# Shared second products as a 512- and a 256-column matmul, read out two banks at a time

## The chip, the cores and the metric

One NeuronCore of a Trainium2 chip runs the kernel. The metric is the device time of one execution in microseconds. Three runs of the kernel before took 1114.66, 1115.58 and 1115.99 us; the median is 1115.58 us.

## The reference

`x` has 128 samples of 64 rows and 256 columns. The first half of the work is a gated mixture of three two-layer networks, in float32:

```python
def _dense(x, wi_, wo_):
    return relu(x @ wi_) @ wo_                 # 256 -> 1024 -> 256
s0 = _dense(x, swi[0], swo[0])                 # shared by all samples
s1 = _dense(x, swi[1], swo[1])
eo = relu(x @ wi[type_label]) @ wo[type_label] # one of 5 experts per sample
gate_in = concat([eo[:, 0], s0[:, 0], s1[:, 0]])
w = softmax(relu(gate_in @ g1) @ g2)           # three weights per sample
x = x + eo * w0 + s0 * w1 + s1 * w2
```

The second half adds to `x` a weighted second difference along the columns, one along the rows (both reflected at the edges), and `zR * x * (1 - x)`.

## The kernel before, in words

Every operand of a product is cut into a high part of reduced precision and a low rest, and the product is the sum of high x high, high x low and low x high. So each logical product is three matmuls, or a wide and a narrow one where the high and low part of the moving operand lie side by side.

The work is a row of passes. Passes 0 and 1 compute the gate's inputs, passes 2 to 23 the expert of one group of samples each and store the results to DRAM. From pass `FIRST` = 24 on come the shared passes: tile t (8 samples, 512 rows, t = 0 to 15) has a pass with b = 0 (`s0`) and one with b = 1 (`s1`), and the last one is split into two passes of half width (`HALVES`). A pass has eight chunks c = 0 to 7 of 128 hidden values. Each engine runs its own program over the same sequence of chunks (`for g in range(G + LAG)`), and semaphores tie them together; the order in each queue is the order of the code.

In 29 of the shared passes (`seven(n)`, all but the first two and the half-width ones) the first product of a pair of chunks is done with seven block products in place of eight, from sums of column blocks of `x` and of weights (`seven_step`). The even step of TensorE holds the products `corner`, `side`, `other` and `corner`, the odd step `other`, `corner` and, last, `corner` for the bottom half. ScalarE copies intermediate banks to SBUF, VectorE adds to them. The even chunk is the "top", the odd chunk the "bottom". Its hidden values come from two places: the right half from `LOW_RIGHT` in SBUF, the left half from the corner bank in PSUM. ScalarE writes the high part (`right_high`, `left_high`), VectorE the low part (`right_low`, `left_low`).

The second product of a chunk follows two steps later (`LAG`): four blocks of 128 rows, in groups (0, 1) and (2, 3) between the products above. In an odd step they stand behind `other` and `corner`; only in step c = 1 do blocks 0 and 1 (of chunk 7 of the pass before) stand first. In the shared passes a block's second product is `pair_product`: three matmuls of 256 columns into half a bank, two blocks per bank. A pass uses two of the four result banks, and the passes alternate between the pairs of banks. `add_shared` multiplies a bank by the sample's weight and adds it to `y`, straight from PSUM, 512 columns at a time: in step c = 2 for a finished b = 1 pass, in c = 5 for a finished b = 0 pass. In the expert passes the second product is a matmul of 512 columns and one of 256 into a bank of its own.

Beside this VectorE has one larger task in most steps: `lap_x`, `react`, `add_x`, `lap_y`, `result` of the previous tile in passes with b = 0, and in passes with b = 1 `turn_tile` (c = 0), `residual` (c = 1), `tile_low_whole` (c = 2), `column_sums` and `column_sums_left` (c = 3 and 4, four operations of 256 columns) and `column_sums_low` (c = 6). ScalarE has `tile_high_whole` in c = 1 and `column_sums_high` in c = 5 of these, and `quadratic` in c = 3 of passes with b = 0. GpSimd issues the expert weights' DMAs in the first stage, then makes two sets of weight sums and two small matrices, and is idle until the last block. SyncE's queue issues the other DMAs; `halos` copies rows of `y` between partitions once `add_shared` of the tile is done.

Of the kernel before, what the change touches and what calls it, by code (L numbers as in the profile page):

```python
# [5 lines left out]
F32 = mybir.dt.float32  # L6
# [135 lines left out]
def acc_before(n, u):  # L142
    return max([v for (m, w), v in ACC.items() if m < n and result_bank(m, w) == result_bank(n, u)], default=0)
# [133 lines left out]
def cond_resid_program(nc, x, itok, zx, zy, zr, wi, wo, swi, swo, g1, g2, out):  # L277
    eo_d = nc.dram_tensor("eo_scratch", (NS + NSLOT, S, D), F32, kind="Internal").ap()
    ctx = ExitStack()
    with ctx:  # L280
# [83 lines left out]
        E0 = sb("e0", [128, D])  # L364
        z1 = sb("z1", [128, 2, 128])
# [11 lines left out]
        acc = [ctx.enter_context(nc.psum_tensor(f"acc{i}", [128, 512], F32)) for i in range(4)]  # L377
# [39 lines left out]
        p_hi = sem("p_hi")  # L417
        p_lo = sem("p_lo")
# [33 lines left out]
        P5_ROOM, LOW_RIGHT = gate_room[:, 0:256], later_part[:]  # L452
# [19 lines left out]
        def acc_of(n, j):  # L472

            if paired(n):
                return acc[result_bank(n, j // 2)][:, j % 2 * D:(j % 2 + 1) * D]
            return acc[result_bank(n, j)][:, 0:D]
# [91 lines left out]


# [23 lines left out]
        def _(e):  # L593
# [134 lines left out]
            def column_sums(t):  # L728

                x = [[by_half(XZ[:])[:, k, 2 * h:2 * h + 2, :] for h in range(2)] for k in range(2)]  # L730
                e.wait_ge(xt_lo, t + 1)
                e.tensor_tensor(x[1][1], x[1][1], x[0][1], ALU.subtract).then_inc(*V.up())
                e.wait_ge(dve_seq, V.n)
                e.tensor_tensor(x[0][1], x[0][1], x[0][0], ALU.subtract).then_inc(*V.up())

            def column_sums_left(t):
                x = [[by_half(XZ[:])[:, k, 2 * h:2 * h + 2, :] for h in range(2)] for k in range(2)]
                e.wait_ge(dve_seq, V.n)
                e.tensor_tensor(x[0][0], x[1][1], x[0][0], ALU.add).then_inc(*V.up())
                e.wait_ge(dve_seq, V.n)  # L740
                e.tensor_tensor(x[1][0], x[1][0], x[0][0], ALU.subtract).then_inc(*V.up())
                AT["columns", t] = V.n

# [19 lines left out]
            def right_low(g):  # L763

                e.wait_ge(p_hi, pair_at(g) + 1)
                e.scalar_tensor_tensor(h_slot(HL, g)[:, 256:512], LOW_RIGHT, 0.0,
                                       h_slot(HH, g)[:, 256:512].bitcast(F32), ALU.max, ALU.subtract).then_inc(p_lo, 1)

            def left_low(g):
                n, c = CHUNKS[g]  # L770
                e.wait_ge(h_hi, g + 1 - 2 * NC)
                e.scalar_tensor_tensor(h_slot(HL, g)[:, 0:256], corner_bank(n, c // 2)[:, 0:256], 0.0,
                                       h_slot(HH, g)[:, 0:256].bitcast(F32), ALU.max, ALU.subtract).then_inc(h_lo, 1)
# [17 lines left out]
            def low_right_sum(g):  # L791
                q = pair_at(g)
                e.wait_ge(p_copy, 4 * q + 4)
                e.tensor_tensor(LOW_RIGHT, LOW_RIGHT, P5_ROOM, ALU.add).then_inc(p_sum, 1)  # L794
# [79 lines left out]
            def add_shared(n):  # L874

                t, b = PASSES[n][1] // 2, PASSES[n][1] % 2
                for u in results(n):
                    y = inner(t)[:, 2 * u:2 * u + 2, :]
                    e.wait_ge(acc_done, ACC[n, u])
                    if b == 0:  # L880
                        e.wait_ge(dve_seq, AT["residual", t])
                    else:
                        e.wait_ge(acc_free, ACC[n - 1, u])
                    e.scalar_tensor_tensor(y, acc[result_bank(n, u)][:].rearrange("p (j d) -> p j d", j=2),
                                           WB[:, 1 + b, t:t + 1], y, ALU.mult, ALU.add).then_inc(acc_free, 1)
# [49 lines left out]
            def shared_sum(j):  # L935
# [3 lines left out]
                e.wait_ge(acc_free, ACC[NP - 3, j // 2])  # L939
                e.scalar_tensor_tensor(y, acc_of(NP - 2 + j % 2, j), WB[:, 2, NT - 1:NT], y, ALU.mult, ALU.add).then_inc(*V.up())  # L940
# [73 lines left out]
            for g in range(G + LAG):  # L1014
# [20 lines left out]
                if (n, c) == (FIRST, 7):  # L1035
                    e.wait_ge(t_prod, T_AT["hidden"])
                    e.tensor_scalar(z1[:].rearrange("p a n -> p (a n)"), tbank[:, 0:256], 0.0, None,
# [8 lines left out]
                if g < G and c == 0 and seven(n - 1) and not seven(n):  # L1046
                    right_low(g - 1)
                    left_low(g - 1)
# [32 lines left out]
                if FIRST <= n < NP - 1:  # L1081
                    t, b = PASSES[n][1] // 2, PASSES[n][1] % 2
                    if b == 0 and t >= 1:
# [17 lines left out]
                    if b == 1 and t < NT - 1:  # L1101
# [29 lines left out]
        def _(e):  # L1131
# [240 lines left out]
            def pair_product(n, j, c):  # L1372
# [3 lines left out]
                to = acc_of(n, j)  # L1376
                if c == 0 and j % 2 == 0:
                    e.wait_ge(acc_free, acc_before(n, j // 2))
                e.matmul(to, hi, woc[:, f, 0:D], start=(c == 0 and j % 2 == 0), stop=False, skip_group_check=True)  # L1379
                e.matmul(to, hi, woc[:, f, D:2 * D], start=False, stop=False, skip_group_check=True)  # L1380
                return e.matmul(to, lo, woc[:, f, 0:D], start=False, stop=(c == NC - 1 and j % 2 == 1),  # L1381
                                skip_group_check=True)

            def half_product(n, j, c):
# [3 lines left out]
                to = acc_of(n, j)  # L1388
# [73 lines left out]
        def _(e):  # L1462
# [31 lines left out]
            def column_sums_high(t):  # L1494
                e.wait_ge(dve_seq, AT["columns", t])
# [11 lines left out]
            def right_high(g):  # L1507
# [3 lines left out]
                e.activation(h_slot(HH, g)[:, 256:512], LOW_RIGHT, ACT.Relu).then_inc(p_hi, 1)  # L1511

            def left_high(g):
                n, c = CHUNKS[g]
                e.wait_ge(h_prod, g + 1)
                e.wait_ge(*h_free(g - NH))
                e.activation(h_slot(HH, g)[:, 0:256], corner_bank(n, c // 2)[:, 0:256], ACT.Relu).then_inc(h_hi, 1)
# [6 lines left out]
            def seven_step(g):  # L1524
# [4 lines left out]
                if c % 2 == 0:  # L1529
# [4 lines left out]
                    if q >= 1:  # L1534
                        right_high(g - 1)
# [4 lines left out]
                    if q >= 1:  # L1540
                        left_high(g - 1)
# [4 lines left out]
                if q >= 1:  # L1546
                    e.wait_ge(p_lo, q)
                e.activation(LOW_RIGHT, corner, ACT.Copy).then_inc(p_copy, 1)  # L1548
                top_high(g - 1)

            def evacuate(n):
                i = PASSES[n][1]
                for j in block_order(n):
# [3 lines left out]
                    e.activation(EO[i % 2][:, j, :], acc[j][:, 0:D], ACT.Copy).then_inc(acc_hi, 1)  # L1557

# [361 lines left out]
```

## Time and profile before

| | |
|---|---|
| median of three runs | 1115.58 us |
| the profiled execution | 1114.96 us |
| its span | 1113.5 us |
| TensorE busy | 1105.2 us, 99%, 8004 matmuls |
| VectorE busy | 819.9 us, 74% |
| ScalarE busy | 593.9 us, 53% |
| GpSimd busy | 89.4 us, 8% |
| granted clock, mean | 0.998 |

The span runs from the first to the last instruction; about 1.5 us of the execution lie outside it. Busy time is a share of the whole span, so an engine can be busier than that in one stage. A matmul's recorded time covers its way through the array and overlaps the next one's; what a matmul costs in a full stream is the distance between two starts. A row's bracket tells how long the engine was idle before it and what released it. hh and hl are the high and low parts of the hidden values, swo and ewo the second weights, acc the result banks, first_part and gT the rooms of the tops, later_part the bottom's right half.

### The profile page before, as it was taken

Reading aid. Unit: us, or ns where it says so; the run is one execution under the profiler, and the core shown is the slowest. Engines: PE = TensorE matmul, PEld = TensorE weight load, DVE = VectorE, ACT = ScalarE, POOL = GpSimd, SP = SyncE. Lnnn points to the kernel's source line nnn. Section 1 sums busy time; section 2 is a strip of 40 time slices with the busy share of each in tenths; the row PEclk is TensorE's granted clock in tenths of the full one; section 3 lists DMA queues with packets and bytes.
Section 4 is the critical chain, followed back from the end, with each engine's and each line's share of the span. In section 5 each row is a group of like instructions: output and inputs, shape, how many; then the busy total and the mean of one; then the engine's idle time right before and its main releaser. Section 6 shows DMA issues by size and latency. Waiting matters only on the chain.

```text
span 1113.5 us, 22306 instructions
## 1 busy us (share of the span) xinstructions
PE 1105.2 (99%) x8004; PEld 1044.5 (94%) x8004; DVE 819.9 (74%) x1459; ACT 593.9 (53%) x1265; POOL 89.4 (8%) x131
## 2 busy tenths in 40 slices
PE   9999999999999999999999999999999999999998
PEld 8888888888888888999999999999999999999998
DVE  5665666666666644787788788787787887877876
ACT  3554555555565532455555555555555555555552
POOL 1211212121121104000000000000000000000001
PEclk9999999999999999999999999999999999999999
DMA  8555656555564425220220221211212212212100
GB/s 271 181 164 180 188 189 195 183 172 169 187 204 147 146 51 165 62 76 32 61 65 30 77 48 50 77 43 56 77 40 58 77 36 62 77 33 64 59 30 25
DMA packets 112368, 114.28 MB, mean 103 GB/s; under 512 B 78505, under 2 KB 87298, under 8 KB 112258
## 3 DMA queue, kind: packets, MB, share of 16 engines
q1 hardware_dynamic: 97826, 61.74, 19.2%
q0 software_dynamic: 13952, 50.60, 14.2%
q8 instruction: 63, 1.03, 0.4%
q10 hardware_dynamic: 480, 0.53, 0.2%
q14 instruction: 47, 0.39, 0.1%
HBM read 91.49 MB, written 17.04 MB: 97 GB/s over the span
## 4 chain that ended last, share of the span: by engine, by line
PE 99%; DVE 1%; issue 0%; ACT 0%; POOL 0%; DVEq 0%; POOLq 0%
PE acc L1380 11%; PE acc L1381 11%; PE acc L1379 11%; PE acc L1365 10%; PE hbank L1286 6%; PE hbank L1287 6%; PE hbank L1229 6%; PE hbank L1230 6%; PE hbank L1231 6%; PE hbank L1288 6%; PE acc L1366 5%; PE tbank L1287 2%; PE tbank L1286 2%; PE tbank L1288 2%; PE acc L1267 1%; PE acc L1342 1%
## 5 line engine op out<-in xcount | busy, mean ns | idle before, releaser
L1380 PE MATMUL acc<-swo,hh 128*128 128x256 f32 x992 | 280.5, 283 | 0.0
L1381 PE MATMUL acc<-swo,hl 128*128 128x256 f32 x992 | 280.2, 282 | 0.0
L1379 PE MATMUL acc<-swo,hh 128*128 128x256 f32 x992 | 279.9, 282 | 0.0
L859 DVE SCALAR_TENSOR_TENSOR hl<-hbank,hh 128x512 fp32r<-128x512 f32 (+1 forms) x184 | 111.7, 609 | 147.6 <-ACT hh L1492 147.4
L1492 ACT ACTIVATE hh<-hbank 128x512 fp32r<-128x512 f32 (+1 forms) x184 | 98.0, 535 | 190.5 <-PE hbank L1231 189.3
L1380 PEld LDWEIGHTS acc<-swo,hh 128*128 128x128 f32 x992 | 189.1, 191 | 0.6
L1381 PEld LDWEIGHTS acc<-swo,hl 128*128 128x128 f32 x992 | 189.5, 191 | 0.0
L1379 PEld LDWEIGHTS acc<-swo,hh 128*128 128x128 f32 x992 | 188.7, 190 | 0.7
L1365 PE MATMUL acc<-ewo,hh 128*128 128x512 f32 x496 | 179.9, 394 | 0.0
L1366 PE MATMUL acc<-ewo,hl 128*128 128x256 f32 x496 | 139.0, 280 | 0.0
L1365 PEld LDWEIGHTS acc<-ewo,hh 128*128 128x128 f32 x496 | 93.1, 188 | 21.1
L1229 PE MATMUL hbank<-xh,ewh 128*128 128x512 f32 (+1 forms) x288 | 107.3, 372 | 0.0
L1230 PE MATMUL hbank<-xl,ewh 128*128 128x512 f32 (+1 forms) x288 | 104.7, 364 | 0.0
L1231 PE MATMUL hbank<-xh,ewl 128*128 128x512 f32 (+1 forms) x288 | 104.3, 362 | 0.0
L1366 PEld LDWEIGHTS acc<-ewo,hl 128*128 128x128 f32 x496 | 93.4, 188 | 4.2
L794 DVE TENSOR_TENSOR later_part<-later_part,gT 128x256 f32<-128x256 f32 x116 | 49.2, 424 | 25.8 <-ACT later_part L1548 24.8
L1548 ACT ACTIVATE later_part<-hbank 128x256 f32<-128x256 f32 x58 | 22.4, 385 | 81.3 <-PE hbank L1288 81.3
L1229 PEld LDWEIGHTS hbank<-xh,ewh 128*128 128x128 f32 x288 | 54.1, 188 | 10.0
L1231 PEld LDWEIGHTS hbank<-xh,ewl 128*128 128x128 f32 x288 | 54.1, 188 | 9.5
L1230 PEld LDWEIGHTS hbank<-xl,ewh 128*128 128x128 f32 x288 | 54.5, 189 | 4.5
L890 DVE TENSOR_TENSOR ewo<-rw,ewo 128x1024 fp32r<-128x1024 f32 x44 | 53.5, 1217 | 2.4 <-ACT ewo L1574 2.4
L1751 POOL TENSOR_TENSOR ss<-y 128x254 f32<-128x254 f32 x3 | 1.8, 609 | 663.2 <-DVE y L940 663.2
(325 smaller groups left out, 2752.4 us busy)
## 6 DMA issues: line engine op xcount, KB each, us to landing
rw<-in_L_cond_wi POOLq DMA_DIRECT2D x44, 512.0 KB, 4.6
rw<-in_L_cond_wo POOLq DMA_DIRECT2D x44, 512.0 KB, 4.6
eo_scratch<-eo SPq DMA_DIRECT2D x128, 64.0 KB, 2.2
rw<-in_x SPq DMA_DIRECT2D x256, 32.0 KB, 2.2
xs<-in_x SPq DMA_DIRECT2D x16, 512.0 KB, 3.5
ei<-eo_scratch SPq DMA_DIRECT2D x16, 512.0 KB, 4.3
xs<-in_x SPq DMA_DIRECT2D x126, 64.0 KB, 3.3
out<-ot SPq DMA_DIRECT2D x15, 512.0 KB, 2.7
```

The costliest lines, as they stand in the source:

```text
L859: e.scalar_tensor_tensor(h_slot(HL, g), bank[:, 0:w], 0.0, h_slot(HH, g).bitcast(F32), ALU.max, ALU.subtract).then_inc(h_lo, 1)
L1229: e.matmul(to, wh[:, k, cs], xh[k], start=(k == 0), stop=False)
L1230: e.matmul(to, wh[:, k, cs], xl[k], start=False, stop=False)
L1231: i = e.matmul(to, wl[:, k, cs], xh[k], start=False, stop=(k == 1))
L1286: e.matmul(to, hi, cols[0], start=start, stop=False, skip_group_check=True)
L1287: e.matmul(to, hi, cols[1], start=False, stop=False, skip_group_check=True)
L1365: e.matmul(acc[j][:, 0:2 * D], HH[:, g % NH, at], woc[:, f, :], start=(c == 0), stop=False)
L1366: m = e.matmul(acc[j][:, D:2 * D], HL[:, g % NH, at], woc[:, f, 0:D], start=False, stop=last)
L1379: e.matmul(to, hi, woc[:, f, 0:D], start=(c == 0 and j % 2 == 0), stop=False, skip_group_check=True)
L1380: e.matmul(to, hi, woc[:, f, D:2 * D], start=False, stop=False, skip_group_check=True)
L1381: return e.matmul(to, lo, woc[:, f, 0:D], start=False, stop=(c == NC - 1 and j % 2 == 1), skip_group_check=True)
L1492: e.activation(h_slot(HU if upright(g) else HH, g), bank_of(g)[:, 0:w], ACT.Relu).then_inc(h_hi, 1)
```

## The change

- `pair_product` issues two matmuls per block in place of three, of 512 and 256 columns, into a bank of its own. A shared pass so fills all four banks, and chunk 0 of the next pass waits until they are read out.
- The read-out has two steps for two banks at a time: `shared_high` on ScalarE copies the high columns, scaled, to `EOS` (in the room of `g1s`); `shared_low` on VectorE adds the scaled low columns. They run in steps c = 1 and c = 2 of the next pass. `add_shared` now adds `EOS` to `y` in SBUF, 1024 columns at once, in the steps where it stood.
- The bottom's hidden values are gathered in one SBUF room `LOW` of 512 columns: ScalarE copies the left half there and cuts the whole with one Relu (`bottom_high`), VectorE makes the low part in one operation (`bottom_low`). Both stand where `left_high` and `left_low` stood.
- `column_sums` moves from VectorE to GpSimd.
- On GpSimd the second set of weight sums moves behind the wait for the gate's hidden values and the two small matrices.
- Waits for the end of `add_shared` (`lap_x`, `quadratic`, `halos`) are on VectorE's own counter.

```diff
-def result_bank(n, u):
-    if paired(n):
-        return 2 * ((n - FIRST) % 2) + u
-    if n in HALVES:
-        return {0: 2, 2: 3, 1: 0, 3: 1}[u]
-    return u
+def result_banks(n, u):
+    return {2 * u, 2 * u + 1} if paired(n) else {u}
 def acc_before(n, u):
-    return max([... if m < n and result_bank(m, w) == result_bank(n, u)], default=0)
+    return max([... if m < n and result_banks(m, w) & result_banks(n, u)], default=0)
...
+        P5_ROOM, LOW = later_part[:], ez[:]
+        def acc_part(u, part):
+            return acc_all[:, 2 * u:2 * u + 2, part * D:(part + 1) * D]
+        EOS = g1s[:, 1:5, :]
...  VectorE
-            def right_low(g): ...
-            def left_low(g): ...
+            def bottom_low(g):
                 e.wait_ge(h_hi, g + 1 - 2 * NC)
+                e.scalar_tensor_tensor(h_slot(HL, g), LOW, 0.0, h_slot(HH, g).bitcast(F32),
+                                       ALU.max, ALU.subtract).then_inc(h_lo, 1)
             def seven_step(g):
                 if c % 2 == 0:
                     top_left_sum(g)
                     if pair_at(g) >= 1:
-                        right_low(g - 1)
-                        left_low(g - 1)
+                        bottom_low(g - 1)
                     return
                 top_right_sum(g)
+                if c == 1:
+                    shared_low(n - 1, 0)
                 low_right_sum(g)
                 top_low(g - 1)
+            def shared_low(n, u):
+                t, b = PASSES[n][1] // 2, PASSES[n][1] % 2
+                e.wait_ge(acc_hi, ACC[n, u] - 2)
+                if (t, b) != (0, 0):
+                    e.wait_ge(dve_seq, AT["shared", t + b - 1, 1 - b])
+                e.scalar_tensor_tensor(EOS[:, 2 * u:2 * u + 2, :], acc_part(u, 1), WB[:, 1 + b, t:t + 1],
+                                       EOS[:, 2 * u:2 * u + 2, :], ALU.mult, ALU.add).then_inc(acc_free, 1)
             def add_shared(n):
-                for u in results(n):
-                    ...
-                    e.scalar_tensor_tensor(y, acc[...], WB[:, 1 + b, t:t + 1], y, ...).then_inc(acc_free, 1)
+                e.wait_ge(acc_free, ACC[n, 1])
+                e.wait_ge(dve_seq, AT["residual", t] if b == 0 else AT["shared", t, 0])
+                e.tensor_tensor(inner(t), inner(t), EOS, ALU.add).then_inc(*V.up())
...  VectorE's order
+                if FIRST < n < NP - 1 and c == 2:
+                    shared_low(n - 1, 1)
                 if g < G and seven(n):
                     seven_step(g)
...
+                    if n > FIRST and not seven(n) and c == 1:
+                        shared_low(n - 1, 0)
...
-                        if c == 3:
-                            column_sums(t + 1)
-                        if c == 4:
-                            column_sums_left(t + 1)
...  TensorE, pair_product
-                e.matmul(to, hi, woc[:, f, 0:D], start=(c == 0 and j % 2 == 0), stop=False, ...)
-                e.matmul(to, hi, woc[:, f, D:2 * D], start=False, stop=False, ...)
-                return e.matmul(to, lo, woc[:, f, 0:D], start=False, ...)
+                e.matmul(acc[j][:, 0:2 * D], hi, woc[:, f, :], start=(c == 0), stop=False)
+                return e.matmul(acc[j][:, D:2 * D], lo, woc[:, f, 0:D], start=False, stop=(c == NC - 1))
...  ScalarE
-            def right_high(g): ...
-            def left_high(g): ...
+            def bottom_high(g):
+                e.wait_ge(h_prod, g + 1)
+                e.activation(LOW[:, 0:256], corner_bank(n, c // 2)[:, 0:256], ACT.Copy).then_inc(p_left, 1)
+                e.wait_ge(p_left, q + 1)
+                e.wait_ge(p_sum, 3 * q + 3)
+                e.wait_ge(*h_free(g - NH))
+                e.activation(h_slot(HH, g), LOW, ACT.Relu).then_inc(h_hi, 1)
             def seven_step(g):
                     e.activation(TOP[q % 2][:, 0:256], corner, ACT.Copy).then_inc(p_copy, 1)
-                    if q >= 1:
-                        right_high(g - 1)
                     ...
                     e.activation(P5_ROOM, other, ACT.Copy).then_inc(p_copy, 1)
                     if q >= 1:
-                        left_high(g - 1)
+                        bottom_high(g - 1)
+            def shared_high(n, u):
+                e.wait_ge(acc_done, ACC[n, u])
+                if (t, b) == (0, 0):
+                    e.wait_ge(t_free, T_AT["spread"])
+                else:
+                    e.wait_ge(dve_seq, AT["shared", t + b - 1, 1 - b])
+                e.activation(EOS[:, 2 * u:2 * u + 2, :], acc_part(u, 0), ACT.Copy,
+                             scale=WB[:, 1 + b, t:t + 1]).then_inc(acc_hi, 1)
...  ScalarE's order
+                if FIRST < n < NP - 1 and c in (1, 2):
+                    shared_high(n - 1, c - 1)
                 if g < G and seven(n):
                     seven_step(g)
...  GpSimd
+            weight_sums(0)
             e.wait_ge(t_free, T_AT["hidden"])
             ... the two small matrices ...
+            weight_sums(1)
+            for t in range(1, NT):
+                column_sums(t)    # four tensor_tensor of 256 columns, each behind the one before
...  SyncE
             def halos(t):
-                e.wait_ge(acc_free, ACC[FIRST + 2 * t + 1, 1])
+                e.wait_ge(dve_seq, AT["shared", t, 1])
```

## Rows read from the trace of the kernel before

**Rows 1.** The page: TensorE's busy time, and the chain of waits by engine.
```profile
PE 1105.2 (99%) x8004; PEld 1044.5 (94%) x8004; DVE 819.9 (74%) x1459; ACT 593.9 (53%) x1265; POOL 89.4 (8%) x131
...
PE 99%; DVE 1%; issue 0%; ACT 0%; POOL 0%; DVEq 0%; POOLq 0%
```
**Rows 2.** Busy us (instructions) of PE, PEld, DVE, ACT, POOL; clock, DMA share, GB/s.
```profile
520.00:1060.00 540.00, 540.00 (x4539) 540.00 (x4538) 446.37 (x835) 304.22 (x745) 0.00 (x0) 1.00 0.20 57
```
**Rows 3.** Timeline, TensorE, an expert pass: start, duration (us), line, operands.
```profile
301.26 0.40 PE L1365 MATMUL acc<-ewo,hh 128*128 128x512 f32 x1
...
302.65 0.40 PE L1229 MATMUL hbank<-xh,ewh 128*128 128x512 f32 x1
```
**Rows 4.** Timeline, TensorE, from pass b = 0 into b = 1.
```profile
697.02 0.28 PE L1288 MATMUL hbank<-th,suml 128*128 128x256 f32 x1
...
698.92 0.28 PE L1379 MATMUL acc<-swo,hh 128*128 128x256 f32 x1
...
699.52 0.28 PE L1381 MATMUL acc<-swo,hl 128*128 128x256 f32 x1
...
702.51 0.28 PE L1379 MATMUL acc<-swo,hh 128*128 128x256 f32 x1
...
703.58 0.28 PE L1379 MATMUL acc<-swo,hh 128*128 128x256 f32 x1
```
**Rows 5.** Timeline, ScalarE, the same stretch.
```profile
697.34 0.39 ACT L1539 ACTIVATE gT<-hbank 128x256 f32<-128x256 f32 x1
697.62 0.38 ACT L1517 ACTIVATE hh<-tbank 128x256 fp32r<-128x256 f32 x1
...
700.84 0.62 ACT L1522 ACTIVATE hh<-first_part 128x512 fp32r<-128x512 f32 x1
701.36 1.06 ACT L1484 ACTIVATE xh<-rw 128x1024 fp32r<-128x1024 f32 x1
```
**Rows 6.** Timeline, VectorE, the same stretch.
```profile
698.03 0.42 DVE L772 SCALAR_TENSOR_TENSOR hl<-tbank,hh 128x256 fp32r<-128x256 f32 x1
...
700.27 0.42 DVE L789 TENSOR_TENSOR first_part<-hbank,first_part 128x256 f32<-128x256 f32 x1 [0.66 <-PE hbank L1288]
...
701.49 0.69 DVE L760 SCALAR_TENSOR_TENSOR hl<-first_part,hh 128x512 fp32r<-128x512 f32 x1
702.10 1.28 DVE L897 SCALAR_TENSOR_TENSOR y<-ei,wb,xs 128x1024 f32<-128x1024 f32 x1
```
**Rows 7.** Groups by form: busy us, mean ns, idle before. ScalarE 100:440, VectorE 520:1060.
```profile
L1492 ACT ACTIVATE hh<-hbank 128x512 fp32r<-128x512 f32 x94 | 56.1, 601 | 110.8 <-PE hbank L1231 110.5
...
L884 DVE SCALAR_TENSOR_TENSOR y<-acc,wb,y 128x512 f32<-128x512 f32 x50 | 35.1, 743 | 0.0
...
L923 DVE TENSOR_TENSOR ss<-y 128x1024 f32<-128x1024 f32 x13 | 15.8, 1216 | 0.0
...
L732 DVE TENSOR_TENSOR rw<-rw 128x256 f32<-128x256 f32 x13 | 5.4, 419 | 0.0
```
**Rows 8.** Timeline, GpSimd and VectorE at the end of the kernel.
```profile
1105.60 0.61 POOL L1751 TENSOR_TENSOR ss<-y 128x254 f32<-128x254 f32 x1 [4.06 <-DVE y L940]
1105.63 0.87 DVE L980 SCALAR_TENSOR_TENSOR qq<-y,sm,qq 128x256 f32<-128x256 f32 x1
...
1106.75 0.47 DVE L980 SCALAR_TENSOR_TENSOR qq<-y,wb,qq 128x256 f32<-128x256 f32 x1
```
**Rows 9.** Timelines, VectorE and TensorE, the gate's weights.
```profile
435.95 2.66 DVE L832 TENSOR_SCALAR wx<-mask,vals 128x16 f32<-128x16 f32 x3
...
438.75 0.43 PE L1432 MATMUL tbank<-wx,selb 128*128 128x96 f32 x2 [2.26 <-DVE wx L832]
```
**Rows 10.** Timelines, the halo copies of one tile (SP's queue) and their reader.
```profile
683.73 0.56 SPq L1820 DMA_DIRECT2D y<-y  x1
...
690.42 0.59 SPq L1832 DMA_DIRECT2D y<-y  x1
...
693.02 1.22 DVE L923 TENSOR_TENSOR ss<-y 128x1024 f32<-128x1024 f32 x1
```

More of the change, by code:

```diff
@@ L142, in acc_before @@
 def acc_before(n, u):
-    return max([v for (m, w), v in ACC.items() if m < n and result_bank(m, w) == result_bank(n, u)], default=0)
+    return max([v for (m, w), v in ACC.items() if m < n and result_banks(m, w) & result_banks(n, u)], default=0)
 def tile_parts(n, c):
@@ L363, in cond_resid_program @@
         g1s = sb("g1s", [128, 6, D])
-        E0 = sb("e0", [128, D])
-        z1 = sb("z1", [128, 2, 128])
+        ez = sb("ez", [128, 2 * D])
+        E0, z1 = ez[:, 0:D], ez[:, D:2 * D].rearrange("p (a n) -> p a n", a=2)
         selb = sb("selb", [128, 128])
@@ L376, in cond_resid_program @@
         tbank = ctx.enter_context(nc.psum_tensor("tbank", [128, 512], F32))
-        acc = [ctx.enter_context(nc.psum_tensor(f"acc{i}", [128, 512], F32)) for i in range(4)]
+        acc_all = ctx.enter_context(nc.psum_tensor("acc", [128, 4, 512], F32))
+        acc = [acc_all[:, i, :] for i in range(4)]
         h_prod = sem("h_prod")
@@ L416, in cond_resid_program @@
         p_sum = sem("p_sum")
-        p_hi = sem("p_hi")
-        p_lo = sem("p_lo")
+        p_left = sem("p_left")
+        x_sum = sem("x_sum")
         raw_in = [sem(f"raw_in{i}") for i in range(2)]
@@ L726, in tile_low_whole @@
                                 ALU.subtract).then_inc(xt_lo, 1)
[L728 to L742, printed above, removed]
             def column_sums_low(t):
@@ L793, in low_right_sum @@
                 e.wait_ge(p_copy, 4 * q + 4)
-                e.tensor_tensor(LOW_RIGHT, LOW_RIGHT, P5_ROOM, ALU.add).then_inc(p_sum, 1)
+                e.tensor_tensor(LOW[:, 256:512], LOW[:, 256:512], P5_ROOM, ALU.add).then_inc(p_sum, 1)
             def seven_step(g):
@@ L872, in evacuate @@
                     e.tensor_tensor(dst, acc[j][:, D:2 * D], dst, ALU.add).then_inc(acc_free, 1)
+            def shared_low(n, u):
[5 more added lines that the diff above has]
+                                       EOS[:, 2 * u:2 * u + 2, :], ALU.mult, ALU.add).then_inc(acc_free, 1)
             def add_shared(n):
                 t, b = PASSES[n][1] // 2, PASSES[n][1] % 2
-                for u in results(n):
[L878 to L885, printed above, removed]
+                e.wait_ge(acc_free, ACC[n, 1])
+                e.wait_ge(dve_seq, AT["residual", t] if b == 0 else AT["shared", t, 0])
+                e.tensor_tensor(inner(t), inner(t), EOS, ALU.add).then_inc(*V.up())
+                AT["shared", t, b] = V.n
             def cut_low(ws, p):
@@ L938, in shared_sum @@
                 e.wait_ge(acc_done, ACC[NP - 2 + j % 2, j])
-                e.wait_ge(acc_free, ACC[NP - 3, j // 2])
-                e.scalar_tensor_tensor(y, acc_of(NP - 2 + j % 2, j), WB[:, 2, NT - 1:NT], y, ALU.mult, ALU.add).then_inc(*V.up())
+                e.wait_ge(dve_seq, AT["shared", NT - 1, 0])
+                e.scalar_tensor_tensor(y, acc[j][:, 0:D], WB[:, 2, NT - 1:NT], y, ALU.mult, ALU.add).then_inc(*V.up())
                 AT["last", j] = V.n
@@ L1494, in column_sums_high @@
             def column_sums_high(t):
-                e.wait_ge(dve_seq, AT["columns", t])
+                e.wait_ge(x_sum, 4 * t)
                 if t >= 3:
@@ L1588, in quadratic @@
             def quadratic(t):
-                e.wait_ge(acc_free, ACC[FIRST + 2 * t + 1, 1])
+                e.wait_ge(dve_seq, AT["shared", t, 1])
                 if t == 0:
@@ L1722, in _, with weight_sums @@
                             EO[u % 2][b:128:k, 0:k // 2, :]).then_inc(last_out, 16)
-            for i in range(2):
+            def weight_sums(i):
                 top, bottom = W_RAW[i]
@@ L1734, in _, with column_sums @@
                 e.tensor_tensor(top[:, 1, :], top[:, 1, :], top[:, 0, :], ALU.subtract).then_inc(w_sum, 1)
+            def column_sums(t):
+                x = [[by_half(XZ[:])[:, k, 2 * h:2 * h + 2, :] for h in range(2)] for k in range(2)]
+                e.wait_ge(xt_lo, t + 1)
+                e.tensor_tensor(x[1][1], x[1][1], x[0][1], ALU.subtract).then_inc(x_sum, 1)
+                e.wait_ge(x_sum, 4 * t - 3)
+                e.tensor_tensor(x[0][1], x[0][1], x[0][0], ALU.subtract).then_inc(x_sum, 1)
+                e.wait_ge(x_sum, 4 * t - 2)
+                e.tensor_tensor(x[0][0], x[1][1], x[0][0], ALU.add).then_inc(x_sum, 1)
+                e.wait_ge(x_sum, 4 * t - 1)
+                e.tensor_tensor(x[1][0], x[1][0], x[0][0], ALU.subtract).then_inc(x_sum, 1)
+            weight_sums(0)
             e.wait_ge(t_free, T_AT["hidden"])
@@ L1823, in halos @@
             def halos(t):
-                e.wait_ge(acc_free, ACC[FIRST + 2 * t + 1, 1])
+                e.wait_ge(dve_seq, AT["shared", t, 1])
                 shifted(t)
```

43 lines of the change are left out of this document (9 added, 34 removed).

## The prediction

> **What bounds the kernel now.** I read the page first: TensorE is busy 99% of the span and the chain of waits ends on it for 99% [rows 1]. Then busy time by stretch: from 520 to 1060 us TensorE starts 4539 matmuls in 540.00 us without a hole, all of 256 columns, so one costs 119 ns; VectorE is busy 83%, ScalarE 56%, GpSimd 0%, and the granted clock is 1.00, the 2.4 GHz level [rows 2]. So a shorter matmul stream shortens the kernel one for one, but only as long as each wait inside it is met in time. So the timelines of TensorE, ScalarE and VectorE around one change of pass decide: what is ready when, and by how much before it is used [rows 4 to 6].
>
> **Fewer matmuls.** A shared second product is three matmuls of 256 columns: 3 x 119 = 357 ns. The new pair, 512 and 256 columns, already exists in the expert passes: four pairs take 302.65 - 301.26 = 1.39 us, 348 ns each [rows 3]. That saves 9 ns on each of 31 passes x 8 chunks x 4 blocks = 992: **-8.9 us**. (Bounds from the rounding of these rows: -7 to -11.)
>
> The Trainium skill (TensorE: Matmul & The Clock Gate, "Wait — 56ns, not 53.3ns?") puts the fixed cost of a warm matmul at about 2.5 ns. One matmul less would then save 2.5 us in all. The rows say 9 ns and I follow them.
>
> **The bottom half of the hidden values.** Before, ScalarE cut the right half early (L1511) and the left half (L1517) right after the copy of `other` (L1539); VectorE's L772 ended at 698.03 + 0.42 = 698.45, and TensorE used the result at 698.92 [rows 4 to 6]. After, everything follows the copy of `other`: a copy of the left half to SBUF, a 512-column Relu that waits for that copy on its own engine, a 512-column subtraction, and only then TensorE. The chain starts when the matmul of 697.02 ends, 697.30:
> - ScalarE copy of `other` from 697.34 [rows 5]; the next one 0.28 later, 697.62, takes 0.38: 698.00.
> - Relu over 512 columns, 0.62 as L1522 [rows 5], after a step of 0.04: 698.66.
> - VectorE over 512 columns, 0.69 as L760 [rows 6], after a step of 0.03: 699.38.
> - to the first matmul 0.14: L832 ends at 435.95 + 2.66 = 438.61 and its reader starts at 438.75 [rows 9]. Ready 699.52.
>
> TensorE wants it at 698.92, less four blocks x 9 ns: 698.88. In step c = 1 the blocks 0 and 1 of the previous pass's last chunk stand first in the queue, so TensorE stops for 0.64 us. Of 29 seven-product passes 28 follow another one: 28 x 0.64 = **+17.9 us**. In the other odd steps six matmuls stand ahead (0.71): wanted 699.59, margin 0.07, which I count as no stall. Bounds: if a dependent step overlapped as independent ones do and the wide operations cost no more than narrow ones, the chain would be some 0.6 shorter and nothing would be lost; if each of four steps is 0.05 longer, it is 0.84 per pass and 0.13 in each of 87 other pairs.
>
> **One set of result banks.** Before, passes alternated between two pairs of banks and the read-out had a pass of time. After, each pass fills all four, so chunk 0 of the next pass must wait for ScalarE's copy and VectorE's multiply-add of banks 0,1 and of banks 2,3. In TensorE's queue blocks 2,3 of chunk 0 stand 703.58 - 698.92 = 4.66 after the blocks above, 4.60 with faster pairs. Behind the new start 699.52 they are wanted at 704.12. Into a pass with b = 1:
> - banks 0,1 done: the row of 699.52 lies 0.60 after 698.92, with pairs 0.58; plus 0.28: 700.38. ScalarE copies 512 columns in 0.60 [rows 7]: 701.02.
> - VectorE: `top_right_sum` (L789, 700.27 [rows 6], later by the stall's 0.60 and earlier by two pairs) 700.85 to 701.27, first read-out (0.74 [rows 7]) to 701.93, `low_right_sum` to 702.27, L760's work 702.19 to 702.88; each starts 0.08 before the last one ends, as 701.49 + 0.69 against 702.10 shows [rows 6]. Then `residual`, 1.28 [rows 6], to 704.08, and only then the second read-out, 704.00 to 704.74; with 0.14: 704.88.
>
> ScalarE's second copy, behind L1484 (1.06 [rows 5]), ends near 703.5 and is not the last. Stall 0.76 us; of such passes there are 14: **+10.6 us**. Banks 0,1 (wanted 703.07, free 701.93) are in time. Into a pass with b = 0 there is no `residual`: the second read-out ends at 703.54, no stall. What is queued behind that wait is all of TensorE, and nothing of another engine gains. Bounds: 0, if VectorE is ahead by the length of `residual`; 1.3 per pass if it comes one 0.7 operation later.
>
> **VectorE's load.** Per tile it gains two additions of 1024 columns (2 x 1.22), loses four column sums (4 x 0.42) [rows 7] and in eight pairs trades 2 x 0.42 for 0.69: 2.4 - 1.7 - 1.2 = -0.5 us of 43. Its busy time falls a little, but in each pair it stands about 1 us at the head of its queue waiting for the Relu, where L766 and L772 were. With two additions of 1.2 to 1.3 per pair it is then full, with 0.05 to 0.1 to spare; I count nothing, it belongs to the range.
>
> **Column sums on GpSimd.** Four operations of 256 columns at about 0.61 to 0.72 end long before ScalarE reads them, so they replace VectorE's for free. But while GpSimd ran L1751 from 1105.60 to 1106.21, VectorE's L980, which reads two SBUF tensors, took 0.87; alone it took 0.47 [rows 8]. So such an operation stands until GpSimd's has ended. In c = 3 the 512-column subtraction, with some 0.4 of slack, is held 0.6: 0.2 lost per tile, x 14 = **+2.8 us**. Bounds: 0; four holds of 0.6 with nothing to cover them, 34.
>
> The Trainium skill (SBUF — State Buffer, "Who interferes with whom") says the same: a VectorE instruction with two SBUF inputs and a GpSimd one that reads SBUF exclude each other for a whole instruction. By that rule, the trace agrees.
>
> **The two ends of the shared stage.** The second set of weight sums now stands behind a wait and the small matrices. In the trace the gate's three L832 take 2.66 us beside GpSimd's sums and TensorE waits 2.26 for them [rows 9]; I expect -2.3. Against it, the first read-out, in pass 25: ScalarE has a copy, a Relu (0.60 each) and three casts of 1.06 ahead of the second copy; wanted 1.9 and 3.4 us after banks 0,1 are done, free at 2.7 and 5.5: stalls 0.7 + 2.1. Net **+0.5**. Into the first half-width pass (a chunk there is 12 matmuls): banks 0,1 wanted at 1.25, free at 2.17; banks 2,3 wanted 0.36 later, free at 4.03 behind `residual`: **+2.4**. Bounds for both: -2 and +6.
>
> **Hidden.** The halo copies now start behind the addition instead of the read-out, some 0.7 us later against TensorE. The last is issued 690.42 - 683.73 = 6.7 after the first, and L923 reads them at 693.02 [rows 10]; the stalls give back 0.6 to 1.4 of it. Zero.
>
> **Sum.** -8.9 + 17.9 + 10.6 + 2.8 + 0.5 + 2.4 = +25.3. The profiled execution took 1114.96 us (span 1113.5), 0.6 below the median 1115.58; so the median should become **1141 us**.
>
> **Rivals.**
> - *Faster.* The bottom chain is under 1.58 us (it was 1.3 in the old order, worked out 2.22), so that 698.88 is met: no 17.9, and VectorE, free 0.6 earlier in each pair, does `residual` in time. Left: -8.9 + 0.5 + 2.4 = -6.0: 1110. For it: dependent operations might overlap. Against it: L1517 ends at 698.00 and its reader L772 starts at 698.03 [rows 5, 6], and the two 512-column operations alone take 1.31.
> - *Only the bottom chain.* VectorE runs ahead by more than 0.76 and the read-out is hidden: 1115.6 + 14.7 = 1130. For it: VectorE idles before L789 at 700.27 for 0.66 [rows 6]. Against it: the chain above leaves that idle time in and is still late.
> - *VectorE full.* The margins of 0.05 to 0.1 in the other pairs don't hold; 0.1 in each of 87 is +8.7, with the longer steps at each pass +5: 1155. For it: 83% busy before and a new 1 us wait per pair. Against it: when it is late, the Relu is already done and the wait vanishes.
> - *The saving fails to show.* In this stream, between 256-column products, the pair costs what three matmuls cost, 357 ns, and the stalls stay: 1141 + 8.9 = 1150. For it: 119 ns is itself measured only among 256-column matmuls. Against it: the expert passes hold the same pair at 348. The page's fixed cost, cited above, stands on this side.
>
> **Numbers.** Forecast 43%, with its own range 1135 to 1148; only the bottom chain 16%; VectorE full 27%; no saving 4%; faster 8%; 2% for an unforeseen near-zero. Range 1124 to 1160. A change under 0.2% (2.2 us) can't be told from none here: faster 0.08, same 0.02, slower 0.90.
>
> **What would show it.** Right: TensorE idle before the first second product of step c = 1 by about 0.6, released by VectorE's 512-column subtraction; before the third block of chunk 0 in b = 1 passes by about 0.8, released by the read-out behind `residual`; four new matmul pairs in 1.39 us; two-input VectorE operations of 1.2 us beside GpSimd's sums. Wrong: TensorE without holes in the shared stage, or holes in every pair.

## The result, and the profile after

| | before | after |
|---|---|---|
| median (lowest to highest), us | 1115.12 (1113.49 to 1115.99) | 1151.97 (1151.12 to 1152.39) |
| span of the profiled execution, us | 1113.5 | 1149.6 |

The ratio is 1.0331, with an interval of 1.0313 to 1.0349: the change costs 36.9 us. The forecast was 1141, a cost of 25.3. The direction and the place of the large holes came out as forecast, the size 11 us too small: 1152 lies above the forecast's own range (1135 to 1148).

The page of after, TensorE's row and the others', and the chain of waits by engine:
```profile
PE 1120.6 (97%) x7012; PEld 996.3 (87%) x7012; DVE 823.0 (72%) x1314; ACT 660.2 (57%) x1327; POOL 140.7 (12%) x191
...
PE 85%; DVE 6%; ACT 3%; issue 3%; SPq 1%; DMA 1%; POOLq 0%; DVEq 0%; POOL 0%; ACTq 0%
```
There are 992 matmuls fewer than in [rows 1]; the chain now leaves TensorE for 15% of its length. The stretches (columns as in [rows 2]) tell where: the first line is the start of the shared stage, the second its body, which had no hole before.
```profile
439.00:453.00 14.00, 8.36 (x30) 6.22 (x29) 10.35 (x15) 5.68 (x8) 5.76 (x5) 0.76 0.25 38
...
520.00:1060.00 540.00, 527.66 (x3570) 478.24 (x3570) 429.49 (x676) 344.78 (x762) 40.11 (x48) 1.00 0.20 54
```
In the body 12.3 of 540 us are idle. The waits, over the whole span (waiting engine and line, releaser, total us, count, longest):
```profile
DVE hl L747 <- ACT hh L1490: 71.0, 94, 1.2
...
PEld acc L1356 <- DVE hl L747: 19.8, 28, 0.7
...
PE acc L1356 <- DVE hl L747: 10.6, 28, 0.4
...
PE acc L1356 <- DVE g1s L856: 9.4, 16, 4.0
PEld acc L1356 <- DVE g1s L856: 8.7, 15, 2.1
```
The 28 waits for the 512-column subtraction (L747, `bottom_low`) and the 14 for the read-out (L856) in the body are the two forecast. VectorE itself stood idle before that subtraction 94 times, waiting for ScalarE's Relu (L1490). A wait is also split here between weight load and matmul, so the sums are not holes; below, holes are differences between starts of matmuls.

From the two traces I took the time at which the last second product of each pass starts, and how much later it is after than before:

| stretch | forecast, us | after minus before, us |
|---|---|---|
| up to the start of the shared stage | 0 | +0.1 |
| the gate's weights | -2.3 | -4.2 |
| the first read-out | +2.8 | +8.23 |
| each of 14 passes b = 0 | +0.64 - 0.29 = +0.35 | +0.58 |
| each of 14 passes b = 1 | +0.64 + 0.76 + 0.2 - 0.29 = +1.31 | +1.38 |
| these 28 together | +23.2 | +27.45 |
| into the half-width passes | +2.4 | +0.19 + 3.94 |

0.29 is the forecast for a pass's 32 pairs; the -0.9 of the three other passes belongs to the lines around them. The right column sums to 35.7; the spans differ by 36.1 and the medians by 36.9.

**The bottom chain.** ScalarE, VectorE and TensorE of after, from a b = 0 pass into a b = 1 pass (as [rows 4 to 6]):
```profile
800.87 0.39 ACT L1510 ACTIVATE later_part<-hbank 128x256 f32<-128x256 f32 x1 [0.32 <-PE hbank L1266]
801.15 0.38 ACT L1486 ACTIVATE ez<-tbank 128x256 f32<-128x256 f32 x1
801.56 0.64 ACT L1490 ACTIVATE hh<-ez 128x512 fp32r<-128x512 f32 x1
```
```profile
802.22 0.69 DVE L747 SCALAR_TENSOR_TENSOR hl<-ez,hh 128x512 fp32r<-128x512 f32 x1 [0.22 <-ACT hh L1490]
```
```profile
802.08 0.40 PE L1356 MATMUL acc<-swo,hh 128*128 128x512 f32 x1
802.32 0.28 PE L1357 MATMUL acc<-swo,hl 128*128 128x256 f32 x1
802.97 0.49 PE L1356 MATMUL acc<-swo,hh 128*128 128x512 f32 x1 [0.37 <-DVE hl L747]
803.30 0.28 PE L1357 MATMUL acc<-swo,hl 128*128 128x256 f32 x1
```
The copy (0.38), the Relu (0.64) and the subtraction (0.69) run one behind the other. Without the wait the third matmul would start at 802.44, 0.12 after the one before. It starts 0.53 later, and its partner comes 0.33 after it instead of 0.24: 0.10 more. That is 0.63, against 0.64 forecast.

**The read-out.** The same pass 5 us on, VectorE and then TensorE:
```profile
806.33 1.28 DVE L876 SCALAR_TENSOR_TENSOR y<-ei,wb,xs 128x1024 f32<-128x1024 f32 x1
807.53 0.74 DVE L856 SCALAR_TENSOR_TENSOR g1s<-acc,wb,g1s 128x512 f32<-128x512 f32 x1
```
```profile
808.33 0.50 PE L1356 MATMUL acc<-swo,hh 128*128 128x512 f32 x1 [0.27 <-DVE g1s L856]
808.67 0.28 PE L1357 MATMUL acc<-swo,hl 128*128 128x256 f32 x1
```
`residual` (L876) stands ahead of the second read-out, as forecast. This hole is 0.43 + 0.10. Three matmuls ahead of it, at 807.44, another of 0.08 + 0.10 was not forecast: ScalarE's copy out of the bank that this matmul writes comes late (14 such waits in the trace, for L1506), because the 1024-column `tile_high_whole` (L1459, 1.05) and its second read-out copy (0.68) stand ahead of it. Together 0.71, against 0.76.

**The port.** By this the text means that VectorE's operations with two SBUF inputs and GpSimd's operations hold each other up. GpSimd's column sums, with the VectorE operations that run beside them:
```profile
810.54 0.74 POOL L1722 TENSOR_TENSOR rw<-rw 128x256 f32<-128x256 f32 x1 [41.23 <-DVE xl L722]
811.36 0.80 POOL L1724 TENSOR_TENSOR rw<-rw 128x256 f32<-128x256 f32 x1
812.24 1.06 POOL L1726 TENSOR_TENSOR rw<-rw 128x256 f32<-128x256 f32 x1
```
```profile
805.40 0.41 DVE L769 TENSOR_TENSOR ez<-ez,later_part 128x256 f32<-128x256 f32 x1
805.73 0.68 DVE L741 SCALAR_TENSOR_TENSOR hl<-first_part,hh 128x512 fp32r<-128x512 f32 x1
...
810.71 0.85 DVE L769 TENSOR_TENSOR ez<-ez,later_part 128x256 f32<-128x256 f32 x1
811.49 1.21 DVE L741 SCALAR_TENSOR_TENSOR hl<-gT,hh 128x512 fp32r<-128x512 f32 x1
```
The same two lines of VectorE take 0.41 and 0.68 when GpSimd is quiet, and 0.85 and 1.21 beside it. TensorE loses 0.10 + 0.10 by the second: 0.2, as forecast, though half of it is the slower start behind a hole and not the wait.

### The profile page after: what moved, and what is told of

It reads as the page before. It is cut to its first block, busy times and chain, and to the rows that moved or that the text cites. A ratio compares the mean times of both kernels' runs of the same rounds, so it can differ in the third digit from the quotient of the medians.

```text
span 1149.6 us, 20274 instructions
## 1 busy us (share of the span) xinstructions
PE 1120.6 (97%) x7012; PEld 996.3 (87%) x7012; DVE 823.0 (72%) x1314; ACT 660.2 (57%) x1327; POOL 140.7 (12%) x191
## 4 chain that ended last, share of the span: by engine, by line
PE 85%; DVE 6%; ACT 3%; issue 3%; SPq 1%; DMA 1%; POOLq 0%; DVEq 0%; POOL 0%; ACTq 0%
PE acc L1356 17%; PE acc L1343 10%; PE acc L1357 8%; PE hbank L1207 6%; PE hbank L1208 6%; PE hbank L1209 6%; PE hbank L1264 5%; PE hbank L1266 5%; PE hbank L1265 5%; PE acc L1344 5%; PE tbank L1264 2%; PE tbank L1265 2%; PE tbank L1266 2%; DVE g1s L856 2%; DVE hl L747 2%
## 5 line engine op out<-in xcount | busy, mean ns | idle before, releaser
L1356 PE MATMUL acc<-swo,hh 128*128 128x512 f32 x992 | 374.8, 405 | 20.1 <-DVE hl L747 10.6
L1356 PEld LDWEIGHTS acc<-swo,hh 128*128 128x128 f32 x992 | 186.8, 188 | 62.9 <-DVE hl L747 19.8
L747 DVE SCALAR_TENSOR_TENSOR hl<-ez,hh 128x512 fp32r<-128x512 f32 x116 | 80.3, 692 | 72.3 <-ACT hh L1490 71.0
L1722 POOL TENSOR_TENSOR rw<-rw 128x256 f32<-128x256 f32 x15 | 12.0, 799 | 586.7 <-DVE xl L722 586.7
L1490 ACT ACTIVATE hh<-ez 128x512 fp32r<-128x512 f32 x116 | 73.5, 634 | 3.7
L1537 ACT ACTIVATE g1s<-acc,wb 128x512 f32<-128x512 f32 x62 | 42.4, 685 | 52.5 <-PE acc L1357 46.0
L1510 ACT ACTIVATE later_part<-hbank 128x256 f32<-128x256 f32 x116 | 44.7, 385 | 28.5 <-PE hbank L1266 28.5
L741 DVE SCALAR_TENSOR_TENSOR hl<-gT,hh 128x512 fp32r<-128x512 f32 x58 | 47.4, 817 | 16.1 <-ACT hh L1495 16.1
```

The costliest lines, as they stand in the source:

```text
L747: e.scalar_tensor_tensor(h_slot(HL, g), LOW, 0.0, h_slot(HH, g).bitcast(F32), ALU.max, ALU.subtract).then_inc(h_lo, 1)
L1356: e.matmul(acc[j][:, 0:2 * D], hi, woc[:, f, :], start=(c == 0), stop=False)
```

## The experiments

Each changes after, unless it says before. Their reference runs are of the kernel before on the same chip. What a pass costs is again read from the starts of its last second product, against before.

**e1: the bottom in two halves again, the rest of the change kept.**
```diff
...  VectorE, seven_step (and the same at the pass behind the last of these)
-                        bottom_low(g - 1)
+                        right_low(g - 1)
+                        left_low(g - 1)
...  ScalarE, seven_step (likewise)
+                    if q >= 1:
+                        right_high(g - 1)
...
-                        bottom_high(g - 1)
+                        left_high(g - 1)
```
`right_high` cuts `LOW[:, 256:512]` behind the copy of the corner, `left_high` the bank's 256 columns behind the copy of `other`.

> The changed kernel with the bottom's hidden values cut in two halves again (right_high, left_high, right_low, left_low as before); all else as changed. Holes theory: the 0.64 us hole before the first second product of step c = 1 goes in 28 passes, -17.9; the read-out hole behind residual stays at about 0.6 in 14 passes: 1133 us. Rival, VectorE full: the holes are VectorE being behind, so the 1 us per pair that it no longer waits for the Relu removes the read-out holes too: 1122 us.

Measured: 1128.70, ratio 1.0127 (1.0106 to 1.0147). A miss, halfway between the two expectations. By the medians 23.3 us of the 36.9 hang on the bottom chain (22.4 by the starts in the traces): more than the 17.9 that its 28 holes make up. A b = 0 pass went from +0.58 to -0.26, which is 0.63 for the hole and about 0.2 for small ones in the other steps; a b = 1 pass went from +1.38 to +0.69. That makes 21.4 in the 28 passes; the half-width passes lost 1.9 less. The read-out's holes stay, where *VectorE full* expected them to go. The waits that stay on the second products are those of the read-out and of the start:
```profile
PE acc L1365 <- DVE g1s L864: 9.6, 16, 4.1
PEld acc L1365 <- DVE g1s L864: 8.9, 15, 2.1
```

**e6: the reverse, before with the new bottom alone.** The edit is e1's turned round, in the kernel before, with the rooms of after: `LOW` is `ez`, the copy of `other` goes to `later_part`.

> The kernel before with only the new way to cut the bottom's hidden values (one room, one Relu, one subtraction). Holes theory: a hole of 0.60 + 0.04 us in 28 passes and nothing else: +18, 1133 us. Rival, VectorE full: the 1 us per pair of waiting for the Relu meets an engine at 83%, holes in many pairs: 1140 us or more. Rival, no effect by itself: 1115 us.

Measured: 1135.06, ratio 1.0175 (1.0159 to 1.0190): +19.8. With all matmuls narrow and the old read-out, the same holes appear:
```profile
PEld acc L1370 <- DVE hl L765: 15.9, 28, 0.6
...
PE acc L1370 <- DVE hl L765: 10.2, 28, 0.4
```
```profile
795.28 0.69 DVE L765 SCALAR_TENSOR_TENSOR hl<-ez,hh 128x512 fp32r<-128x512 f32 x1 [0.27 <-ACT hh L1506]
```
```profile
795.27 0.28 PE L1371 MATMUL acc<-swo,hh 128*128 128x256 f32 x1
795.39 0.28 PE L1372 MATMUL acc<-swo,hl 128*128 128x256 f32 x1
...
796.03 0.38 PE L1370 MATMUL acc<-swo,hh 128*128 128x256 f32 x1 [0.36 <-DVE hl L765]
```
796.03 is 0.52 later than 795.39 + 0.12. So the chain alone carries the largest loss. A b = 1 pass costs 0.61 here, a b = 0 pass 0.81: the small losses of after's b = 0 passes come with the chain too. There are 28 large holes, and no hole in every pair: *VectorE full* is refuted for this part.

**e2: `residual` moved out from ahead of the read-out.**
```diff
-                        if c == 1:
+                        if c == (4 if t < NT - 1 else 3):
                             residual(t)
```


> The changed kernel with residual moved from step c = 1 to c = 4 (c = 3 in the last tile), behind the second read-out. Holes theory: the hole before block 2 of chunk 0 (0.43 + 0.10 us) goes in 14 passes, -7.4, and 1 to 3 us go at the first half-width pass; the hole of c = 1 stays: 1142 us. Rival, VectorE full: the same work at another place, at most 2 us: 1150 us.

Measured: 1148.66, ratio 1.0303 (1.0282 to 1.0324). A miss: 3.3 us came back instead of some 10. And these are at the end: into the half-width passes the cost fell from 3.94 to 1.30, while each b = 1 pass still costs 1.39. The third block of chunk 0 is nearly in time, but the hole stands one pair later. TensorE and VectorE of e2:
```profile
808.02 0.50 PE L1356 MATMUL acc<-swo,hh 128*128 128x512 f32 x1
...
812.83 0.50 PE L1356 MATMUL acc<-swo,hh 128*128 128x512 f32 x1 [0.31 <-DVE hl L741]
```
```profile
811.56 1.22 DVE L741 SCALAR_TENSOR_TENSOR hl<-gT,hh 128x512 fp32r<-128x512 f32 x1
```
The subtraction held by GpSimd (1.22) is the same as in after, and there TensorE came only 0.10 too early for it. What changed is TensorE: no longer stopped for `residual`, it comes 0.4 us sooner to a result that is ready at the same time.

**e3: the column sums back on VectorE**, in c = 3 and c = 4 as before, `residual` as in after.
```diff
+                        if c == 3:
+                            column_sums(t + 1)
+                        if c == 4:
+                            column_sums_left(t + 1)
...  GpSimd
-            for t in range(1, NT):
-                column_sums(t)
```


> The changed kernel with the column sums back on VectorE in steps c = 3 and 4. Port theory: VectorE's operations with two SBUF inputs are no longer held by GpSimd's, the 0.2 us hole per tile goes: -2.9, and 0.5 at the first tile: 1149 us. Rival, VectorE full: 1.7 us more work per tile for an engine without room, 0.3 to 1 us per tile: 1156 to 1166 us.

Measured: 1148.15, ratio 1.0295 (1.0273 to 1.0318), close to the 1149 expected. A b = 1 pass costs 1.16 to 1.23 instead of 1.37 to 1.41; 0.2 over 14 is 2.8 us, the port's forecast. The intervals of e3 and after touch, so the total alone would not settle it; the 14 equal passes do.

**e5: e2 with the column sums left out.**
```diff
                         if c == (4 if t < NT - 1 else 3):
                             residual(t)
...  ScalarE, column_sums_high
-                e.wait_ge(x_sum, 4 * t)
+                e.wait_ge(xt_lo, t + 1)
...  GpSimd
-            for t in range(1, NT):
-                column_sums(t)
```


> The kernel with the late residual (e2), and the column sums left out altogether (one part of the computation is missing). Two causes for one hole: the run with the late residual had its hole of 0.53 us before block 2 of chunk 0 replaced by one of 0.57 in c = 4, behind VectorE's subtraction of c = 3, which GpSimd's column sums held from 0.69 to 1.22. Theory: either cause alone keeps the hole, without both it is gone: 14 x 0.6 less than 1148.7, so 1140 us. Rival, VectorE is full at c = 3 whatever GpSimd does: 1147 us.

Measured: 1142.18, ratio 1.0238 (1.0222 to 1.0253). Now a b = 1 pass costs 0.87. The subtraction that was held takes its usual time:
```profile
808.45 0.69 DVE L740 SCALAR_TENSOR_TENSOR hl<-gT,hh 128x512 fp32r<-128x512 f32 x1 [0.36 <-ACT hh L1494]
```
Moving `residual` alone brought nothing per pass, removing the port's conflict alone 0.2, both together 0.5 (0.6 was expected). Two late results overlap here: each covers for the other. What is left in a b = 1 pass is the bottom's 0.63 and about 0.35 behind ScalarE's late copies, less the shorter pairs.

**e4: before with only the second weight sums moved behind the gate.**
```diff
-            for i in range(2):
+            def weight_sums(i):
                 ...
+            weight_sums(0)
             e.wait_ge(t_free, T_AT["hidden"])
             ... the two small matrices ...
+            weight_sums(1)
```


> The kernel before with one part of the change: the second set of weight sums on GpSimd behind the wait for the gate's hidden values and the two small matrices. Port theory: VectorE's three small L832-type operations take 0.2 instead of 0.9 us each, TensorE's wait of 2.26 us goes, and with it the 3.4 us at half clock (1.7 us): 1111.5 us. Rival: the wait was set by something else, no change: 1115.5 us.

Measured: 1111.69 against 1114.45, ratio 0.9977 (0.9967 to 0.9987), in 12 runs. The three L832 of [rows 9] (2.66) shrink, and the stretch behind them, here in before and then in e4, is at full clock:
```profile
439.00:443.50 4.50, 4.50 (x21) 4.08 (x21) 3.84 (x9) 2.28 (x3) 1.72 (x5) 0.62 0.14 23
```
```profile
436.81 0.55 DVE L832 TENSOR_SCALAR wx<-mask,vals 128x16 f32<-128x16 f32 x3
```
```profile
439.00:443.50 4.50, 4.50 (x32) 4.12 (x31) 0.95 (x1) 2.50 (x3) 3.74 (x3) 1.00 0.18 27
```
21 matmuls started in 4.5 us before, 32 now. So the gate's wait cost its 2.26 us and about 4.5 x 0.38 = 1.7 more in clock (from 440 to 442 it was 0.50, the 1.2 GHz level), together 4.0, and by the starts in the two traces pass 24 is 4.0 shorter; the prediction took only the first. The next pass gives 0.4 back. The medians differ by 2.8 only. Before's 17 runs are not alike: those with a mean clock of 1.000 took 1112.2 to 1112.9 us, the others up to 1117.4 at 0.997. So some may not have lost the clock at the gate; only one is in a trace.

**c3 and c4: what the experiments point to.** Kept from the change: the wide pairs, the two-step read-out, the order at the gate. Undone: the new bottom, the column sums on GpSimd. Moved: `residual` to c = 5 and the addition of the b = 0 pass to c = 7; in the first shared passes, the transpose `turn_tile` to c = 1, behind the copy of the gate's weights, and the casts of the weight sums to c = 3. c4 also gives ScalarE's `tile_high_whole` and what depends on it one step more:
```diff
-                        if c == 1:
+                        if c == (5 if t < NT - 1 else 3):
                             residual(t)
...
-                        if c == 0:
+                        if c == (1 if t == 0 else 0):
                             turn_tile(t + 1)
...  c4 alone, ScalarE and then VectorE
-                    c == (2 if n == FIRST + 1 else 1): tile_high_whole
+                    c == 2: tile_high_whole
...
-                        if c == 2:
+                        if c == (2 if t == 0 else 3):
                             tile_low_whole(t + 1)
-                        if c == 3:
+                        if c == (3 if t == 0 else 4):
                             column_sums(t + 1)
```


> A version from the runs: the matmul pair, the two-step read-out and the gate order of the changed kernel; the bottom in two halves and the column sums on VectorE as before; residual in c = 5 and add_shared of b = 0 passes in c = 7; at the first read-out the transposition behind the gate's weights, the casts of the weight sums behind the read-out. Theory: passes with b = 0 gain 0.22 us each, with b = 1 0.03, the start of the shared stage 2 and its end loses 1: 1110 us. Rival: the read-out finds another engine late and the 0.5 us holes stay: 1118 us.

> c3 with ScalarE's tile_high_whole in step c = 2, behind the second read-out, in place of c = 1, tile_low_whole in c = 3 and both halves of the column sums in c = 4 (first tile as in c3). In c3 a pass with b = 1 still has holes of 0.09 + 0.10 and 0.05 + 0.10 us behind ScalarE's late copies. Theory: these go and all passes gain 0.22: 14 x 0.4 less than c3's 1113.2, 1107.6 us. Rival: VectorE, with 1.2 and 1.7 us in neighbouring steps, is late there and the holes move: 1113 us.

Measured: c3 1113.21 against 1115.24, ratio 0.9984 (0.9975 to 0.9993), 3 us short of the 1110 expected, a b = 1 pass at +0.16 in place of -0.03; c4 1108.53 against 1114.89, ratio 0.9946 (0.9933 to 0.9960). c4 is faster than both kernels, and than e4. Its body:
```profile
520.00:1060.00 540.00, 540.00 (x3770) 501.73 (x3769) 467.08 (x866) 340.65 (x803) 0.00 (x0) 1.00 0.21 57
```
TensorE is full again, with 200 more matmuls started than in after. VectorE is busy for 467 us, 38 more than in after, and TensorE waits for none of it. In c4 the b = 1 passes went from c3's +0.16 to -0.18 against before. The wait that c3 has between 520 and 1060 us, and c4 has not, is for ScalarE:
```profile
PEld tbank L1292 <- ACT gT L1536: 3.2, 13, 0.3
```
So the slack for ScalarE's cast is the likely cause; VectorE's `tile_low_whole` and `column_sums` moved with it, and no run separates them.

## Why the forecast was right in direction and short in size

**Where the total fell.** 1152 is nearest to the 1155 of *VectorE full*, but e1, e6 and the waits above refute its cause. The holes are the forecast's own; what it got wrong is above all the two ends.

**Fewer matmuls: -8.9 forecast, 7 to 8 us gained.** Four pairs of the shared stage in after:
```profile
820.62 0.39 PE L1356 MATMUL acc<-swo,hh 128*128 128x512 f32 x1
...
822.02 0.28 PE L1264 MATMUL tbank<-th,swh 128*128 128x256 f32 x1
```
1.40 us against 12 x 0.119 = 1.43: 7 ns each. The b = 0 passes of e1 and c4, which have no large holes, are 0.24 to 0.28 shorter than before, for 32 pairs: about 8 ns. So *the saving fails to show* is refuted. The figure of the Trainium skill (TensorE: Matmul & The Clock Gate, "Wait — 56ns, not 53.3ns?"), about 2.5 ns for a warm matmul, would give a third of what was measured; the rows decide.

**The bottom half: +17.9 forecast, 28 x 0.63 = 17.6 measured.** The chain's steps come out at 2.14 instead of 2.22 (shorter steps), and the restart of the matmul stream adds 0.10 that I had not counted; the two cancel. That the sum hit is in part luck. *Faster* and *only the bottom chain* fall with e1, e6 and the read-out's hole.

**The margin of 0.07 in the other pairs didn't quite hold.** In b = 0 passes 0.05 and 0.10 are lost in c = 3 and less elsewhere, about 0.2 a pass, and what is left of b = 1 passes is 0.1: some 4 us in all, of which I had counted nothing but had named the size (0.1 in each of 87 would be 8.7). *VectorE full* was wrong in its cause: VectorE waited for the Relu before 94 of these subtractions, and with the new bottom alone (e6) the same 0.2 appear. The chain is late by itself.

**The read-out behind `residual`: +10.6 forecast, 14 x 0.71 = 9.9 measured**, of which 0.18 has another cause (ScalarE). The prediction took 0.60 for ScalarE's scaled copy from a Relu's row; it takes 0.69. As a removable cost it is nothing: e2.

**The port: +2.8 forecast, 2.8 by e3.** The number hit by luck: [rows 8] show 0.40 more (0.87 against 0.47) and not 0.6, the subtraction was held 0.53 (1.21 against 0.68), and of the 0.2 lost 0.10 is the slower start behind the hole, which the prediction didn't have. GpSimd's operations lengthen too, 0.74 to 1.06. The Trainium skill (SBUF — State Buffer, "Who interferes with whom") says that a VectorE instruction with two SBUF inputs contends with a GpSimd instruction that reads SBUF; the trace agrees, with 1.21 against 0.68. For the total it matters only where someone waits for the one held.

**The start: +0.5 forecast, +4.02 measured.** This is the term that failed most. The step read "stalls 0.7 + 2.1" for the first read-out; it was 4.0 and 1.6 of waiting and then half the clock. VectorE, ScalarE and TensorE of after:
```profile
440.68 1.24 DVE L717 STREAM_TRANSPOSE rw<-rw 128x1024 f32<-128x1024 f32 x1 [4.24 <-DMA rw<-in_x]
441.85 0.22 DVE L813 COPY wb<-tbank 128x96 f32<-128x96 f32 x1
```
```profile
442.16 0.69 ACT L1537 ACTIVATE g1s<-acc,wb 128x512 f32<-128x512 f32 x1 [6.51 <-DVE wb L813]
```
```profile
444.86 0.47 PE L1356 MATMUL acc<-swo,hh 128*128 128x512 f32 x1 [4.04 <-DVE g1s L856]
447.59 0.80 PE L1356 MATMUL acc<-swo,hh 128*128 128x512 f32 x1 [1.60 <-DVE g1s L856]
```
ScalarE's copy scales by the gate's weights WB. VectorE copies WB out of a bank behind `turn_tile`, which waits 4.24 us for a transfer of the next tile. That order stood in before as well; there the read-out had a pass of time. I counted what stood ahead of the read-out on ScalarE, but not what its operand waited for. In c3, with `turn_tile` behind that copy, the weights are there early, ScalarE's copy waits for TensorE alone, and the first wait is the 0.7 of the forecast:
```profile
436.96 0.26 DVE L836 COPY wb<-tbank 128x96 f32<-128x96 f32 x1
439.07 0.69 ACT L1569 ACTIVATE g1s<-acc,wb 128x512 f32<-128x512 f32 x1 [3.11 <-PE acc L1385]
441.77 0.47 PE L1384 MATMUL acc<-swo,hh 128*128 128x512 f32 x1 [0.66 <-DVE g1s L879]
```
This stretch costs +1.61 in c3 and +1.65 in c4 instead of +8.23. In both the casts of the weight sums moved as well, so the smaller second wait (0.76 for 1.60) can't be put down to `turn_tile` alone. The gate's own gain was mis-sized the other way: -4.2 for -2.3.

**The end: +2.4 forecast, +4.1 measured.** Two stalls of 0.84 and 1.17 (forecast 0.92 and 1.5), and then the clock, which the prediction left out (4 us at 0.57 cost about 1.7, an estimate):
```profile
1119.58 0.35 PE L1364 MATMUL acc<-swo,hh 128*128 128x256 f32 x1 [0.84 <-DVE g1s L856]
...
1121.34 0.58 PE L1364 MATMUL acc<-swo,hh 128*128 128x256 f32 x1 [1.17 <-DVE g1s L856]
```
```profile
1121.00:1125.00 4.00, 3.66 (x18) 3.66 (x19) 1.54 (x4) 0.38 (x1) 0.00 (x0) 0.57 0.00 0
```

**Sum of the misses.** In the 28 passes 27.45 - 23.2 = 4.2: pairs +1.1, read-out -0.7, bottom -0.3, and so 4.1 for the small holes. At the two ends, with the pairs there, 0.5 + 2.4 - 0.9 = 2.0 was forecast and 4.02 + 4.13 = 8.2 measured: +6.2. With +0.1 ahead of the stage that is 10.5 of the 11.6 missing (36.9 - 25.3). The other 1.1 us lies between the last of these starts and the medians (35.7, 36.1, 36.9), which no row assigns.

## What to carry to other kernels

Where a buffer loses its second copy, follow each operand of the operation that frees it back to its own wait, at the ends of the loop above all, and not only the queue ahead of it. An engine 80% busy says nothing of a chain: three wide operations in a row were late while each half-width pair in parallel was in time. When two results are late for one reader, removing one shows little; take both away before judging either.

## What the runs showed of the hardware

- After a hole in TensorE's stream, the next matmul of 512 columns takes 0.50 instead of 0.40 and its successor starts 0.33 instead of 0.24 later; of 256 columns (e6, 796.03) it takes 0.38 instead of 0.28. A 0.05 us late result so costs 0.15. The weight load of such a matmul starts with it, at 792.42 for the matmul of 792.43 in after, where in the stream it starts earlier, at 792.88 for that of 793.11; that this is the cause was not shown.
- After TensorE had waited 4.04 and 1.60 us, the granted clock was 0.76 on average over 14 us, with 0.50, the 1.2 GHz level, from 446 to 452; after 2.26, it was 0.62 over 4.5 us; after 0.84 and 1.17, 0.57 over 4 us. In c4, after waits of 0.65 and 0.76 in the same place, it stayed at 1.00:
```profile
439.00:453.00 14.00, 12.59 (x63) 10.17 (x62) 11.22 (x17) 7.52 (x11) 3.29 (x3) 1.00 0.24 37
```
- ScalarE's copy of 512 columns out of a bank with a scale per partition takes 0.69 (L1537), the Relu without one 0.60 [rows 7].
